# Dense expert rows of a mixture layer: four groups of four experts as fp32r halves, in an eight-row audio tower on one NeuronCore

## What is computed

```python
h = gelu(gelu(x @ W1 + b1) @ W2 + b2); lens = sigmoid(h @ W3 + b3)      # per token
h = warp(x, lens)                                    # 750 -> 375 tokens
h = h + rmsnorm(linear_attention(layernorm(h)))      # 8 heads of 64
xf = layernorm(h)                                    # all 8*375 tokens
probs = softmax(xf @ switch_w.T + switch_b); routes = argmax(probs)   # 16 experts
pos = rank of the token among those of its expert, in token order; keep = pos < capacity
out = h + where(keep, xf @ expert_w[route].T + expert_b[route], xf) * max(probs)
```

## Time and profile before

| | us |
|---|---|
| median of three runs | 393.56 |
| lowest, highest of them | 393.56, 394.36 |
| span of the profiled execution | 392.4 |
| PE busy | 374.4 (95%) |
| DVE busy | 335.1 (85%) |
| ACT busy | 227.2 (58%) |
| POOL busy | 111.8 (28%) |

### The profile page before, as it was taken

One profiled execution on the slowest core, in us unless ns is written; L12 is line 12 of the kernel. 1 busy time (PEld: TensorE's weight loads), 2 busy tenths in 40 slices (PEclk: granted clock), 3 DMA queues, 4 the chain that ended last, 5 costly groups with the idle time before them and its releaser, 6 DMA issues. The chain is left out here.

```text
span 392.4 us, 7891 instructions
## 1 busy us (share of the span) xinstructions
PE 374.4 (95%) x2702; PEld 327.1 (83%) x2702; DVE 335.1 (85%) x916; ACT 227.2 (58%) x433; POOL 111.8 (28%) x136
## 2 busy tenths in 40 slices
PE   8999899999999999999999999999999989999892
PEld 8887788888889888888988888888887788998892
DVE  4687869969897999799988999899998975888896
ACT  4653369627971699159933994389537743782200
POOL 6121301031152216221522141403330501107880
PEclk9999999999999999999999999999999999999998
DMA  7768002002000110002000200100000070331134
GB/s 222 193 197 272 2 1 85 3 0 82 5 20 3 27 62 22 3 0 85 14 10 1 86 7 15 47 0 3 22 0 0 22 195 7 89 118 33 41 80 126
DMA packets 16406, 21.58 MB, mean 55 GB/s; under 512 B 4930, under 2 KB 11928, under 8 KB 15934
## 3 DMA queue, kind: packets, MB, share of 16 engines
q1 hardware_dynamic: 12398, 18.30, 16.1%
q0 software_dynamic: 2880, 2.35, 2.4%
q10 hardware_dynamic: 1088, 0.42, 0.4%
HBM read 14.40 MB, written 6.62 MB: 54 GB/s over the span
## 5 line engine op out<-in xcount | busy, mean ns | idle before, releaser
L1093 PE MATMUL psB<-W2h,h1l 128*125 128x512 f32 x184 | 74.6, 406 | 0.0
L1094 PE MATMUL psB<-W2l,h1h 128*125 128x512 f32 x184 | 72.5, 394 | 0.0
L1095 PE MATMUL psB<-W2h,h1h 128*125 128x512 f32 x184 | 72.5, 394 | 0.0
L668 ACT ACTIVATE h2b<-h2b 125x512 f32<-125x512 f32 x48 | 30.0, 628 | 30.9 <-DVE h2b L1640 30.5
L1095 PEld LDWEIGHTS psB<-W2h,h1h 128*125 128x125 f32 x184 | 34.1, 185 | 8.5
L1094 PEld LDWEIGHTS psB<-W2l,h1h 128*125 128x125 f32 x184 | 34.2, 186 | 6.9
L1093 PEld LDWEIGHTS psB<-W2h,h1l 128*125 128x125 f32 x184 | 34.2, 186 | 6.9
L1640 DVE TENSOR_TENSOR h2b<-psB,b2r 125x512 f32<-125x512 f32 x48 | 32.8, 685 | 4.5 <-PE psB L1095 4.4
L651 ACT ACTIVATE h<-psA,b1c 128x376 f32<-128x376 f32 x60 | 33.3, 579 | 5.7 <-PE psA L1040 3.9
L1647 DVE CUSTOM_DVE_ANT_0 h2b<-h2b,W3r 125x512 f32<-125x512 f32 x48 | 32.9, 690 | 1.6 <-ACT h2b L668 1.4
L531 POOL TENSOR_TENSOR dx<-xt 125x640 f32<-125x640 f32 x8 | 12.9, 1617 | 64.6 <-PE psC L1118 53.0
(11 more groups left out here) (284 smaller groups left out, 970.0 us busy)
## 6 DMA issues: line engine op xcount, KB each, us to landing
xTf<-in_x_t SPq DMA_DIRECT2D x16, 187.5 KB, 2.5
xt<-in_x SPq DMA_DIRECT2D x8, 336.0 KB
slot_x<-eb_parts SPq DMA_DIRECT2D x2, 960.0 KB, 11.9
basef<-in_L_tok_W SPq DMA_DIRECT2D x4, 256.0 KB, 5.3
ewT<-in_expert_t SPq DMA_DIRECT2D x1, 1024.0 KB, 8.0
ewf<-slot_x SPq DMA_DIRECT2D x2, 480.0 KB, 6.2
h2b<-slot_x SPq DMA_DIRECT2D x2, 480.0 KB, 8.2
slot_y<-h SPq DMA_DIRECT2D x4, 240.0 KB, 2.4
```

Source lines behind the costliest of these rows:

```text
L668: nc.scalar.activation(slot, slot, ACT.Gelu).then_inc(c_g2.sem, 1)
L1093: mm(ps, lo, W2h[:, k, :], start=k == 0, stop=False)
L1094: mm(ps, hi, W2l[:, k, :], start=False, stop=False)
L1095: last = mm(ps, hi, W2h[:, k, :], start=False, stop=k == HK - 1)
```

## The change

What it does:

- The 16 experts of a dense row are taken in four groups of four. For group g, `own_tokens(b, g)` writes the tokens whose expert is in that group, once from the upper and once from the lower half (two fp32r tiles). `dense(b, g)` multiplies them with the group's four matrices side by side, 512 columns, as lower times upper, upper times lower, upper times upper: nine matmuls a group, 36 a row, in place of 48 fp32 matmuls of 128 columns.
- Each token then has four results of 128 columns. `own_rows(b, j)` adds the right one to the base: four operations in a chain for each of the three blocks, each scaled by the token's share (probability or zero). `finish_row` is no longer called for rows 6 and 7.
- Added for it: the halves of the expert matrices (`expert_upper` on ACT, `expert_lower` on POOL, in the tiles of W2), of the turned tokens (`own_upper`, `own_lower`), of the biases (`group_biases`), and the group number, the place in the group and the shares (`group_columns`, more in `spread_choice`, `shares`). The bias matrix is loaded twice, as [4, 512].
- Row 6 has no ring any more. The loops `pipeline`, `step`, `opening` and `ending` are written out as flat lists. Apart from the calls named here the order of each engine's list is as before.

New order at the end. ACT: `expert_upper(0..3)` after `take_kt(6, 2)` and ahead of `take_qt(6, 0)`; `own_upper(6)` and (7) right after `take_xft(6)` and (7). POOL: `expert_lower(0..3)` between `norm1(7)` and `norm2(6)`. PE: `attend(7)`, `dense_bias(6)`, `dense(6, 0)`, `dense(6, 1)`, `xf_transposed(7)`, `dense(6, 2)`, `logits(7)`, `chosen_on_rows(7)`, `dense(6, 3)`, `positions(7)`, `dense_bias(7)`, `dense(7, 0..3)`. DVE, from the end of row 6's attention (`group_columns` stands ahead, after `take_outputs(5)`):

The core of the diff:

```diff
 def spread_choice(b):
-    after(dve, c_rm, b, 1)
+    after(dve, c_oh, b, 1)
+    r = b - PRIOR
+    vec.tensor_tensor(grp[:, r], oh[:], grank[:]...to_broadcast([TP, GJ, E]), ALU.mult).then_inc(s_grp[b], 1)
+    vec.tensor_reduce(place[:, r], oh[:].rearrange("p j (g k) -> p j k g", g=GROUPS), AX.X, ALU.add).then_inc(s_grp[b], 1)
+    dve.wait_ge(s_grp[b], 2)
+    vec.tensor_reduce(gcode[:, r], grp[:, r], AX.X, ALU.max).then_inc(s_grp[b], 1)
+    dve.wait_ge(s_grp[b], 3)
     after(dve, c_h2, b, 1)
-    vec.tensor_copy(rmw[:], rm[:]...).then_inc(s_rmw[b], 1)
+    vec.tensor_copy(rmw[:], gcode[:, r]...).then_inc(s_rmw[b], 1)
+def group_biases():
...
+    vec.tensor_copy(eb_both, ebs[:]).then_inc(s_bias, 1)
+    dve.wait_ge(s_bias, 1)
+    vec.tensor_tensor(eb_both[32:64], ebs[32:64], eb_both[32:64], ALU.subtract).then_inc(s_bias, 1)
+def own_lower(b):
...
+    vec.tensor_tensor(own_l[b], xf_turned(b), own_h[b], ALU.subtract).then_inc(s_own[b], 1)
 def own_tokens(b, g):
-    vec.scalar_tensor_tensor(only[b][e], bank_chosen(b)[:, 0:G], float(E - e), xf_turned(b), ALU.is_equal, ALU.mult)
+    vec.scalar_tensor_tensor(only_h[b][g], bank_chosen(b)[:, 0:G], float(GROUPS - g), own_h[b], ALU.is_equal, ALU.mult)
+    vec.scalar_tensor_tensor(only_l[b][g], bank_chosen(b)[:, 0:G], float(GROUPS - g), own_l[b], ALU.is_equal, ALU.mult)
+def own_rows(b, j):
+    dve.wait_ge(s_dense[b], GJ * (GROUPS - 1) + j + 1)
...
+    for k in range(GROUP):
+        if k:
+            dve.wait_ge(s_mix[b], j * (GROUP - 1) + k)
+        done = s_mix[b] if k < GROUP - 1 else s_res if j == GJ - 1 else s_mixed
+        vec.scalar_tensor_tensor(yg[b][:, j, :], y[:, k * C:(k + 1) * C], share[:, r, j, k:k + 1],
+                                 yg[b][:, j, :] if k else base[:, i, :], ALU.mult, ALU.add).then_inc(done, 1)
 def dense(b, g):
-    pe.wait_ge(s_only[b], e + 2)
+    pe.wait_ge(s_ewh, g + 1)
+    pe.wait_ge(s_ewl, g + 1)
+    pe.wait_ge(s_only[b], 2 * g + 3)
     for j in range(GJ):
-        last = mm(banks_dense(b)[j][0:TP, 0:C], only[b][e][:, j * TP:(j + 1) * TP], ewT[:, e, :], ...)
-    last.then_inc(s_dense[b], 1)
+        ps, of = banks_dense(b)[j][0:TP, :], slice(j * TP, (j + 1) * TP)
+        mm(ps, only_l[b][g][:, of], ew_h[g], start=False, stop=False)
+        mm(ps, only_h[b][g][:, of], ew_l[g], start=False, stop=False)
+        mm(ps, only_h[b][g][:, of], ew_h[g], start=False, stop=g == GROUPS - 1).then_inc(s_dense[b], 1)
+def expert_upper(g):                                  # ACT
+    act.wait_ge(s_ew, 16)
+    after(act, c_l2, LAST, TJ)
+    copy(ew_h[g], ewT[:, GROUP * g:GROUP * (g + 1), :]...).then_inc(s_ewh, 1)
+def expert_lower(g):                                  # POOL
+    pool.wait_ge(s_ewh, g + 1)
+    pool.tensor_tensor(ew_l[g], ewT[:, GROUP * g:GROUP * (g + 1), :]..., ew_h[g], ALU.subtract).then_inc(s_ewl, 1)
```

More of the change, by code:

```diff
@@ L392, in outputs_taken @@
                 eng.wait_ge(s_yb, n)
[L394 to L400, removed]
         @block.sync
@@ new lines, in _ @@
+            k_transposed(7, 6, 1)
+            positions(6, None)
+            k_transposed(7, 6, 2)
+            values(7, 6, 2)
+            q_transposed(7, 6, 0)
+            q_transposed(7, 6, 1)
+            context(7, 6)
+            chosen_on_rows(6)
+            fold(7, 6, None)
+            q_transposed(7, 6, 2)
+            attend(7, 6)
+            dense_bias(6)
+            dense(6, 0)
+            dense(6, 1)
+            xf_transposed(7, None)
+            dense(6, 2)
+            logits(7, None)
@@ L1599, in _ @@
+            chosen_on_rows(7)
+            dense(6, 3)
+            positions(7, None)
+            dense_bias(7)
+            dense(7, 0)
+            dense(7, 1)
+            dense(7, 2)
+            dense(7, 3)
         @block.vector
@@ new lines, in _ @@
+            take_m(1, 0)
+            keep_base(0, None)
+            moments1(2, 1)
+            normal1(2, 1)
+            dot3(3, 2, 0)
+            out_norm(1, 0)
+            xn_lo(2, 1)
+            bias2(3, 2, 1)
+            residual(1, 0)
+            moments2(1, 0)
+            bias2(3, 2, 2)
+            normal2(1, 0)
+            query_max(2, 1, 0)
+            x_lo_next(3)
+            key_max(2, 1, 0)
+            query_max(2, 1, 1)
+            keep_h(2, 1)
+            dot3(3, 2, 1)
@@ new lines, in _ @@
+            key_sum(7, 6)
+            query_norm(7, 6)
+            place_in_expert(6, 5)
+            probability(6, 5)
+            spread_choice(6)
+            keep_base(6, 5)
+            shares(6)
+            group_biases()
+            own_lower(6)
+            own_experts(6)
+            own_tokens(6, 0)
+            take_m(7, 6)
+            own_tokens(6, 1)
+            out_norm(7, 6)
+            own_tokens(6, 2)
+            own_norm2(7, 6)
+            residual(7, 6)
+            moments2(7, 6)
@@ new lines, in _ @@
+            own_norm3(7, 6)
+            normal2(7, 6)
+            own_tokens(6, 3)
+            take_logits(7, 6)
+            route(7, 6)
+            own_counts(7, 6)
+            spread_choice(7)
+            own_lower(7)
+            own_experts(7)
+            own_tokens(7, 0)
+            own_tokens(7, 1)
+            own_rows(6, 0)
+            own_rows(6, 1)
+            own_rows(6, 2)
+            own_tokens(7, 2)
+            finish_row(0)
+            place_in_expert(7, 6)
+            own_tokens(7, 3)
```

1950 lines of the change are left out of this document (1140 added, 810 removed).

## The result

| | before | after |
|---|---|---|
| median of the runs, us | 393.84 (393.56 to 394.36, 4 runs) | 402.12 (401.3 to 405.04, 4 runs) |
| span of the profiled execution | 392.4 | 399.7 |
| that execution's own time | not shown | 401.51 |
| mean granted TensorE clock in that span | 0.996 | 0.987 |

The changed kernel takes 1.0225 times as long, 95% interval [1.0194, 1.0257]. The range of 396.5 to 402.2 holds the median by a hair, but its upper end is 1.0220 times the 393.56 us that the forecast started from, and the measured ratio lies just above that; the value of 399.4 is 2.7 us too low. The runs of after spread over 3.7 us, those of before over 0.8: that was not in the prediction either, and it led to the question of the clock.

The account below looks back on a forecast made before the run. DVE was taken to set the end, by turns with PE from row 6's choice, then alone. 1.9 - 1.4 + 1.4 + 0.6 + 3.4 = +5.9 us gave span 398.3, plus 1.16 outside: 399.4 us, range 396.5 to 402.2.

Parts of the forecast that it names:

- Part one: Up to attend(7): new DVE work ahead of take_m(7), 2.9 us less 0.75 hidden, starts attend(7) 1.9 us later.
- `expert_lower` at 0: POOL's four subtractions before norm2(6), 5 to 7 us long, delay hidden by later work and gaps: 0, upper end 1 us.
- Part two: From out_norm(7) to normal2(7): row 6's masks leave the gaps of this DVE chain, -1.4 us.
- Part three: From logits(7) to the choice: dense(6, 2) ahead of logits +1.4 us, three more operations in spread_choice(7) +0.6 us.
- Part four: Tail from own_experts(7), DVE alone: cheaper masks, but 24 chained own_rows steps at 0.37 us; 19.8 us, +3.4.
- rival B: Chained own_rows steps on DVE cost 0.26 us like independent ones, 2.4 us less in total: 397.0 us, chance 0.10.
- Outside the span, 1.16: Time added to the forecast span: the median before stood 1.16 us above its profiled span, carried over unchanged.
- Rival C: PE's clock falls to half in its 3.5 us gap before row 7's choice and stays low: 405 us, chance 0.05.

Follow-up runs that it names:

- e4: Changed kernel with the four expert_lower subtractions on DVE, in its idle time before moments1(7), instead of POOL: 401.58 us, ratio 1.0193.
- e2: Kernel before with only expert_upper on ACT and expert_lower on POOL added, results unused: 394.85 us, ratio 1.0026.
- e9: Changed kernel with the expert_lower subtractions on DVE before moments1(7) and 27 unread matmuls of ones in PE's three gaps: 400.47 us, ratio 1.0165.
- e8: Changed kernel with 27 unread matmuls of ones filling PE's three late idle stretches: 401.75 us, ratio 1.0188.
- e7: Changed kernel with own_rows' 12 steps alternating over the three independent blocks, so none follows its own predecessor: 400.97 us, ratio 1.0178.
- e5: Changed kernel with take_m(7) right behind group_biases, ahead of own_lower(6), own_experts(6) and the first masks: 399.91 us, ratio 1.0149.
- e6: Changed kernel with logits(7) ahead of dense(6, 2) on PE: 401.84 us, ratio 1.0203.
- e1: Changed kernel with the four expert_lower moved later on POOL, behind counts(6): 403.84 us, ratio 1.025.
- e3: Changed kernel with the four expert_lower moved earlier on POOL, ahead of norm1(7): 404.82 us, ratio 1.0289.

## Why the prediction missed, step by step

**Part one, `attend(7)` +1.9: right in itself.** Measured +3.04; without POOL's work (e4, `attend(7)` at 358.51) it is +1.87.

**`expert_lower` at 0: wrong, the step that failed first.** The length was forecast well (5 to 7 us, measured 4.96). The price was taken from who waits for POOL's next result (`norm2(6)`), and that queue cost nothing: POOL was through at 332.85 and stood idle 0.87 us before `norm2(6)`. The price arose at operations that wait for nothing of POOL: `normal1(7)` beside it took 3.76 us instead of 0.86, the first square of `out_norm(6)` 0.81 instead of 0.29. By that DVE gave `norm2(6)` its input 1.11 us later, and nothing behind absorbed it: `residual(6)` starts 1.11 us later too (335.87 against 334.76). Alone it costs 1.0 us (e2), in the changed kernel 1.3 (e9 against e8). The rest of the stretching goes into the 1.95 us for which DVE stood idle ahead of `out_norm(6)` in before. The upper end of 1 us for POOL in the range was the right size, for another reason.

**Part two, -1.4: measured -1.09.** Right in kind: the three places come to -0.46, -0.34 and -0.55 us, as forecast. The 0.3 is `normal2(7)`, whose three steps take 1.14 us instead of 0.87; one of them lasts 0.81 us and ends with one of POOL's gathers (369.4). No run tests whether that is the cause.

**Part three, +1.4 and +0.6: measured +1.99.** The logits are +1.35. The choice came to +0.64. The three new operations of `spread_choice(7)` take 0.58 us (374.86 to 375.44), as forecast. The clock adds 0.35 (0.89 us instead of 0.54 for the turned choice, gone in e8), and 0.3 comes off that no part of the prediction had: `own_counts(7)` takes 0.75 us instead of 0.95, and `take_logits(7)` comes 0.1 us sooner behind `logits(7)`. That these two cancel is luck.

**Part four, +3.4: measured +3.36.** To the hundredth that is luck, in kind it is right. Both the chained step (0.37 forecast; 0.39 inside a chain, 0.26 at the border of a block) and the order of the engines held; the fallen clock behind the choice did not hold up `own_rows(6)`. By the rule behind rival B (the Trainium skill, VectorE: DVE Perf Modes, The DRAIN you can't avoid), the chained steps would have cost the same as the spread ones; e7 shows 4.26 us against 3.11 for twelve. The trace does not agree.

**Outside the span, 1.16: should have been 1.7.** I subtracted the span of the profiled run from the median of other runs. The runs of before that carry both numbers show 1.7 to 1.8, and so do those of after (401.51 - 399.7). By that the profiled run of before took about 394.1 us, an estimate, 0.5 above the median that I started from. This is 0.6 us of the miss, and it is no change at all.

**Rival C, the clock: right mechanism, wrong place and size.** I weighed it at one gap, that before the choice, and at two outcomes. In fact all three new gaps can bring it down. Behind the one of 3.3 us before the choice it fell in all eight profiled runs that have it, behind one of 2.5 us before `attend(7)` in three of seven, behind the one before the transposes of xf in two of nine (e5; and e6, where it came only in the `dense(6, 2)` that follows). Where it fell behind the choice, DVE's slack swallowed nearly all (0.35 us were left in after). Where it fell in `attend(7)`, which is on the path, it cost 1.4 to 2.6 us (e4, e7, e6, e1). In the unprofiled runs of after, the spans were 399.6, 401.0 and 403.3 at mean clocks of 0.986, 0.982 and 0.979: the longer, the lower. That the clock is the cause there is argued from this order and from e8, whose four runs with fillers are all below 402; no trace of the run of 405.04 exists, so it is not shown. The argument against C, that the clock stayed up for 4 us after the last matmul, was no bound on how soon it falls: here it fell behind a gap of 1.9 us (e5). The Trainium skill (TensorE: Matmul & The Clock Gate, Part 1) has it that an idle array loses the full clock and must earn it back by work; the trace agrees in kind, with 0.50 of full behind some gaps of 1.9 us and more.

The sum: 1.87 (part one) + 1.17 (POOL) - 1.09 (part two) + 1.99 (part three, 0.35 of it the clock) + 3.36 (tail) = 7.3 us of span, where 5.9 was forecast. Of the 1.4 us between them 1.17 is POOL, the step at nothing, and 0.3 part two. With 0.65 more outside it that is the profiled run, 2.1 us above the forecast. The median of 402.12 lies another 0.6 above that run; the two slower runs have lower clocks.

## What to carry to other kernels

When work goes to an engine that has time, look not only at who waits for its result but at what the other engines run on SBUF in that same stretch, and move it to where they are idle or working on PSUM. Where one engine waits for a whole instruction of the other, shorter instructions might make that wait shorter; no run here tries it. When a change makes TensorE faster, the time saved becomes gaps; count those ahead of work on the critical path as a risk of half clock, and close them (here by moving one small DVE operation ahead of four larger ones) or fill them, which held the clock here but gained nothing on its own. Chains of short DVE operations are cheaper when steps of independent chains alternate.

## What the runs showed of the hardware

POOL and DVE hold each other up when both work between SBUF tiles, for most of the kinds of operation met here: three DVE operations of 128 columns (TENSOR_SCALAR) went from 0.86 to 3.76 us, a SCALAR_TENSOR_TENSOR of 1536 columns with two SBUF inputs from 1.73 to 2.62, the warp's two lines (TENSOR_SCALAR) from 3.36 to 5.34, and POOL's own four subtractions took 4.95 to 6.53 us depending on what ran beside them. A TENSOR_REDUCE of 1536 columns stayed at 1.75 us, and operations that read PSUM kept their length (0.55 us). The rows fit a wait for the end of the other engine's current instruction, not a shared rate: 1.30 us for each of three operations beside POOL's 1.26, and 0.77 us for one of 3 columns. So the small operations suffer most by ratio. The same four subtractions on DVE took 2.47 us.

The granted clock fell to 0.50 behind idle stretches of TensorE of 1.9 to 3.3 us, but not behind each of them: in the profiled run of after, the gaps of 2.55 and 1.73 us passed without a fall, and only behind the one of 3.31 did it come. Twenty-four matmuls of `attend(7)` took 2.88 us at full clock and 4.28, 4.34, 4.54 and 5.48 where it fell. In e3 it fell behind a gap of 2.69 us ahead of the warp. What decides whether a gap of 2.5 us brings it down stays open.
